# First attention of a six-stage decoder: output groups after turned tiles 6, 10, 14 and 2, output turn after tile 8, later projections after tile 4

## What is computed

```
x = x + _L0_attn_ref(_layernorm(x, axis=-1), ...)

q1, q2 = jnp.split(q, 2, axis=-1)
k1, k2 = jnp.split(k, 2, axis=-1)
a1 = jax.nn.softmax(jnp.einsum('bhsd,bhtd->bhst', q1, k1) * scale, axis=-1)
a2 = jax.nn.softmax(jnp.einsum('bhsd,bhtd->bhst', q2, k2) * scale, axis=-1)
a = a1 - lam * a2
out = jnp.einsum('bhst,bhtd->bhsd', a, v)
...
out_final = out_cat.transpose(0, 2, 1).reshape(b, s, e)
return out_final @ wo
```

## Time and profile before

| | |
|---|---|
| median of 3 runs | 996.46 us |
| profiled execution, its own time | 997.39 us |
| span of the profiled execution | 995.7 us |
| mean granted TensorE clock | 0.953 |
| PE, DVE, ACT, POOL busy | 90%, 76%, 63%, 46% |
| first attention, steady bodies | about 60 to 358 us of the span |

### The profile page before, as it was taken

One profiled execution on the slowest core, in us unless ns is written; L12 is line 12 of the kernel. 1 busy time (PEld: TensorE's weight loads), 2 busy tenths in 40 slices (PEclk: granted clock), 3 DMA queues, 4 the chain that ended last, 5 costly groups with the idle time before them and its releaser, 6 DMA issues. The chain is left out here.

```text
span 995.7 us, 18196 instructions
## 1 busy us (share of the span) xinstructions
PE 894.6 (90%) x5700; PEld 450.0 (45%) x5732; DVE 755.2 (76%) x1998; ACT 627.4 (63%) x1476; POOL 454.0 (46%) x680
## 2 busy tenths in 40 slices
PE   2899999999999998899979999999999999897496
PEld 1222222222222234565645555555556555576396
DVE  4879989889999966899837688666766866785564
ACT  3379989889999983333256666666666665354164
POOL 4143475554543452111045455545555454685444
PEclk8589999999999999999989999999999999997598
DMA  4116113111129990000070000000000000000340
GB/s 96 26 26 76 26 26 56 26 26 27 26 66 262 249 245 12 1 1 1 1 221 6 9 6 15 9 6 9 9 13 9 6 2 1 1 2 22 96 119 17
DMA packets 64143, 46.12 MB, mean 46 GB/s; under 512 B 22009, under 2 KB 61093, under 8 KB 64048
## 3 DMA queue, kind: packets, MB, share of 16 engines
q1 hardware_dynamic: 62304, 41.24, 18.4%
q0 software_dynamic: 1744, 3.72, 1.1%
HBM read 15.54 MB, written 21.45 MB: 37 GB/s over the span
## 5 line engine op out<-in xcount | busy, mean ns | idle before, releaser
L696 DVE TENSOR_REDUCE a_nmax<-a_rows 128x2 f32<-128x1024 f32 x256 | 298.6, 1216 | 35.7 <-PE a_rows L452 32.7
L933 ACT ACTIVATE a_probs<-a_turned 128x512 f32<-128x512 f32 x512 | 271.6, 606 | 36.6 <-PE a_turned L464 36.4
L1439 POOL TENSOR_TENSOR a_prob<-a_prob,a_rinv 128x256 f32<-128x256 f32 (+3 forms) x128 | 159.7, 1254 | 153.4 <-DVE a_rinv L1698 153.2
L1690 DVE CUSTOM_DVE_ANT_0 a_prob<-a_score,a_past_mask 128x128 f32<-128x128 f32 (+3 forms) x256 | 115.1, 487 | 87.9 <-PE a_score L1485 87.1
L1608 ACT ACTIVATE a_prob<-a_prob,a_nmax 128x128 f32<-128x128 f32 (+3 forms) x256 | 141.2, 553 | 52.7 <-DVE a_nmax L1690 52.6
L464 PE MATMUL a_turned<-a_q,a_qk 32*128 32x512 bf16 x512 | 149.6, 389 | 9.6 <-ACT a_q L953 1.1
L435 PE MATMUL a_acc<-a_probs,a_vg 128*32 128x512 f32 x1024 | 139.6, 618 | 0.0
L452 PE MATMUL a_rows<-a_qk 32*128 32x512 bf16 x512 | 103.5, 402 | 11.6 <-DMA a_qk<-a_lo 8.3
L464 PEld LDWEIGHTS a_turned<-a_q,a_qk 32*128 32x128 bf16 x512 | 35.0, 91 | 169.2 <-ACT a_probs L933 148.3
L1485 PE MATMUL a_score<-a_k_s,a_q_s 64*128 64x384 f32 (+3 forms) x512 | 103.1, 481 | 0.6 <-ACT a_vals L1599 0.5
L1495 PE MATMUL a_turn<-g_ident,a_prob 128*128 128x128 f32 x640 | 97.4, 283 | 3.9 <-DVE a_pt L1704 3.3
(11 more groups left out here) (340 smaller groups left out, 1426.4 us busy)
## 6 DMA issues: line engine op xcount, KB each, us to landing
xs_sorted<-a_blank SPq DMA_DIRECT2D x9, 1935.0 KB, 26.2
m_m_w<-L_ffn_w SPq DMA_DIRECT2D x8, 512.0 KB, 8.6
a_qk<-a_hi SPq DMA_DIRECT2D x192, 16.0 KB, 1.8
c_xs<-xs_sorted SPq DMA_DIRECT2D x23, 129.0 KB, 2.1
a_qk<-a_fill SPq DMA_DIRECT2D x8, 256.0 KB, 7.8
a_qk<-a_mid SPq DMA_DIRECT2D x128, 16.0 KB, 1.8
g_a_wq<-L_attn_Wq SPq DMA_DIRECT2D x32, 64.0 KB, 2.0
g_X<-x SPq DMA_DIRECT2D x4, 256.0 KB, 5.0
```

Source lines behind the costliest of these rows:

```text
L696: dve.tensor_reduce(nmax[i % 2][:, p // 2, (p % 2) * 2:(p % 2) * 2 + 2], rows[n % 2][:, :, :], AX_X, ALU.max, negate=True).then_inc(row_ou ...
L933: act.activation(probs[:, (tb % 2) * 4 + j, :], turned[n % 3][:, :], ACT.Exp, scale=float(HD0) ** -0.5).then_inc(turn_out, 1)
L1439: pool.tensor_tensor(pr, pr, spread(rinv[:, t % RING, :], 2, width), ALU.mult).then_inc(scl, 1)
L1690: dve.tensor_tensor_reduce(out=prob[t % RING][:, j, 0:width], in0=score[t % 2][:, j, 0:width], in1=past_mask[:, S - width:S], scale=-1.0, ...
```

## The change

Three constants and two conditions move instructions on TensorE and, for the ring's items, in the same way on ScalarE. No instruction is added or removed, and the order on VectorE, GpSimd and SyncE is the same as before.

```diff
-        AHEAD, OUT, CUT = 6, 6, 12
-        OUTPUTS = (7, 10, 15, 2)
+        AHEAD, OUT, CUT, AFTER = 6, 8, 12, 4
+        OUTPUTS = (6, 10, 14, 2)
...
-                items += [("later", 0)] if k == 12 and i in LATER else []
+                items += [("later", 0)] if k == AFTER + 1 and i in LATER else []
...
-                    if k == 11 and i in LATER:
+                    if k == AFTER and i in LATER:
                         later_item(i, r)
```

## The result

The changed kernel takes 1003.81 us (median of 4 runs, 1001.85 to 1005.93), the kernel before 996.42 (4 runs, 995.02 to 997.75). The ratio is 1.009, with a 95% interval of 1.0061 to 1.0119: slower by 7.4 us, where the prediction had 7.9. The profiled execution took 1005.93 us with a span of 1004.2.

The account below looks back on a forecast made before the run. TensorE and ScalarE waiting for each other through three `turned` buffers bound the kernel. Even bodies +7.5, odd +3.8, body 31 -0.1, later projections -2.8, body 1 -0.5 make +7.9 us: median 1004.4 us, range 997 to 1010.

Parts of the forecast that it names:

- The loop: TensorE and ScalarE wait for each other through three `turned` buffers; a run of four tiles and its group takes 2.38 us.
- the steps: Adding the loop's lengths tile by tile; on the order of before said to give 19.88 us for the measured 19.90.
- Even bodies: Bodies without output turn: both groups of a half get four tiles ahead; 9.50 to 10.00 us, +0.50 each.
- odd bodies: Bodies with the output turn: +0.33 in the shift's half, -0.06 in the output turn's half, +0.27 each.
- Later projections: Behind tile 4 they cost 0.74 us (even bodies) or 0.79 (odd) instead of 1.17; together 2.8 us saved.
- My bound of 19.0 us for VectorE: VectorE's need in two bodies: 16 maxima of at most 1.17 us and 0.26 us of reciprocal, idling 0.9 us.
- the first rival: Even spacing keeps ScalarE supplied, so the period falls to VectorE's 19.0 us; some 980 us, faster; chance 0.10.
- Rival (2): Each gap between groups comes 0.06 us shorter by faster hand-over behind a lone tile; stays at 997 us; chance 0.12.
- Rival (3): VectorE's cover breaks: tile 5's row pair holds tile 6 back 0.15 us, two gaps a body; 1013 us; chance 0.08.
- The ends: First and last bodies: body 1 -0.5 us (between -1.5 and +1); body 31's second half and body 32 0, within 1.
- rival (4): The clock rises one body earlier or later: 2.5 us either way, within the range; counted in the forecast's 0.70.
- body 31: Near-last body, its second half carrying output projections and cross attention between the tiles; term -0.1 us.

Follow-up runs that it names:

- `shifthalf`: The kernel before with one group moved, the third from tile 15 to tile 14, projections left behind tile 11; 1004.69 us, ratio 1.0101.

## Why the prediction was right, and where its terms were off

**The loop** held in all its lengths: 0.42, 0.66, 0.30 and 1.00 us give 2.38 for a run of four, and the profile after has 2.38 to 2.39. One test of it was weaker than it read. Of the 19.88 us that the steps were said to give for the order of before, only the 4.90 of the shift's half comes from them; 4.59 and 5.49 were read from the rows. By the steps the run of five takes T + 2.86 to the next T, and the half body 4.39. The 0.20 us between that and 4.59 are VectorE's, as the halved maxima show (T + 2.88), so VectorE was not off the path in the kernel before. The Trainium skill (TensorEngine Tiling (Array Packing), section PSUM Bottleneck), by which the PSUM copy may become the bottleneck behind packed matmuls, is not what sets the time here: the waits show both readers of PSUM waiting for TensorE. Only with half groups does VectorE fill its time, 18.35 of 18.35 us, and only with four buffers does ScalarE, 98.90 of 100 us.

**Even bodies** +0.54 (term 0.50) and **odd bodies** +0.34 (term 0.27). Of the 0.07 us missing in the odd body, 0.04 are in the group behind the copy of `acc` (2.61 and not 2.57), the rest 0.01 to 0.02 in each stretch behind the output turn and the shift. Over 28 bodies that is 1.5 us.

**Later projections** in place: 0.74 and 0.76 us (terms 0.74 and 0.79). In the order of before they cost 0.61 and 0.49, so the two parts of the change stand in each other's way by 0.13 and 0.27 us a body.

**VectorE** idle 20.78 - 18.91 = 1.87 us in two bodies, where it was 19.90 - 18.86 = 1.04 (busy time of DVE from one copy of q to the second next). My bound of 19.0 us for VectorE was too high: 15 maxima that ran without a gap with half groups took 17.05 us, 1.14 each, and both bodies 18.3. With the right bound the first rival would have promised less than 980 us, and still not come. The wait that this rival rested on, tile 6 for tile 3, is there (270.71 to 271.79). Rival (2) named the hand-over behind a lone tile; it stayed 0.31 to 0.32 us (271.79 to 272.10, 258.66 to 258.98), not 0.06 shorter. Rival (3) is refuted by the halved maxima: with them the order of after is as long as without.

**The ends** were mis-sized, and they cancel what the bodies add. Body 1 gave -2.3 (term -0.5) and body 2 -0.9 (term +0.1), by the clock's rise; that is rival (4), 2.8 us where it had 2.5. The Trainium skill (TensorE: Matmul & The Clock Gate, section What's actually happening) has throttling as the default and activity as what releases it; the runs agree in part. The rise comes in steady work, but the half groups kept the lower level with TensorE busy 48.23 of 50 us.

For body 31 I took -0.1, and it was +0.56. Of this 0.34 is what every odd body gained, and the rest is in the run with tiles 8 to 10. Timeline of TensorE before, from tile 8 to tile 11, the first one behind the next group,

```profile
360.21 0.39 PE L464 MATMUL a_turned<-a_q,a_qk 32*128 32x512 bf16 x3
...
361.53 0.39 PE L464 MATMUL a_turned<-a_q,a_qk 32*128 32x512 bf16 x1
```

and after, from tile 7 to tile 11:

```profile
366.46 0.39 PE L464 MATMUL a_turned<-a_q,a_qk 32*128 32x512 bf16 x2
...
369.34 0.38 PE L464 MATMUL a_turned<-a_q,a_qk 32*128 32x512 bf16 x1
```

No unit comes behind, so no row pairs stand between the tiles. Before, the short run takes 1.32 us and not 1.54 (260.72 to 262.26); after, the run of four keeps its 2.88, since it waits for the round trip and not for row pairs. What follows body 31 adds 0.7 in sum: ScalarE begins the cross attention (L957) at 376.96 us before and at 384.12 after, 7.16 later, which gives 0.64 back, and the 1.4 us lost behind it fall where the granted clock is lower for longer (0.74 and 1.00 in the two stretches of 5 us from 380 us before, 0.98, 0.50 and 0.83 in three after). That the clock is the cause there is not shown.

So the sum was right at 7.9 for 8.5 us partly by luck: steady bodies 1.4 us more than forecast, body 31 and what follows it another 1.4, body 0 0.7, and the clock's rise 2.8 us the other way. Bodies 3 to 30, at full clock in both profiles, differ by 9.8 us, and executions of like mean clock by 11 (1001.85 to 1003.93 at 0.958 after, 991.67 to 992.49 at 0.958 to 0.959 before, in the rounds of the experiments). So the change costs nearer to 10 us than to 7.4.

**The better version** leaves the groups and the output turn where they were, and takes the later projections behind tile 4: 988.66 us, 6.0 under the kernel before on the same chip, of which the bodies explain 4.4.

## What to carry to other kernels

Where two engines hand tiles round through few buffers, don't space the long instructions of one of them evenly by habit: write down the round trip (hand-over there, hand-over back, the long group) and count how many of its runs have enough tiles in hand to skip it. A short run of tiles that finds every buffer free can be worth more than even gaps. Put rare extra work where a buffer is in hand, and judge each part of such a change by itself: here one part gained 4 to 6 us and the others lost 12 to 14.

## What was not expected of the hardware

With groups of half the length, TensorE's granted clock stayed at 0.50 over long stretches although its record shows it busy 48.23 of 50 us, and a kernel with less work took 1035 to 1049 us for 995. The kernel before has 1.00 between 100 and 350 us, with TensorE busy 231.90 of 250. Busy time in the record does not tell whether the clock will be granted; at the lower level the same products also take longer, so the two shares don't compare work. And executions of the kernel before spread over 5.6 us (991.67 to 997.23 in 19 runs) with their mean granted clock (0.951 to 0.959). The first rise lies between 55 and 60 us in the profile before and near 50 us in those of after and `shifthalf`; that it is what differs between executions of one kernel is not shown.
